# A fused decoder layer: an opening ordered engine by engine, the output bias added by VectorE, and products nobody reads in three recurring waits of TensorE

## The reference

```python
x = x + attn(layernorm(x))                       # one head, width 128, softmax over 256 keys
x = x + xattn(layernorm(x), ctx)                 # 16 heads of 64, 1601 keys; out @ Wo + bo
x = x + ffn_block(layernorm(x))                  # a router takes 31 of 256 rows of each batch
```

```python
q = (x @ Wq).reshape(B, Nq, 16, 64)              # k, v likewise from the context
sim = einsum('bhid,bhjd->bhij', q, k) * SCALE
attn = softmax(sim)
return einsum('bhij,bhjd->bhid', attn, v).reshape(B, Nq, 1024) @ Wo + bo
```

## Time and profile before

| | |
|---|---|
| median of 3 executions | 2245.14 us (2243.27 to 2247.11) |
| the profiled execution: its own time | 2249.61 us |
| its span, first to last instruction | 2248.4 us |
| mean granted TensorE clock | 0.989 |
| busy: PE / ACT / POOL / DVE | 2154.0 / 1831.9 / 1926.4 / 1781.7 us |
| the first score product starts at | 41.00 us |

### The profile page before, as it was taken

The page is one execution under the profiler, slowest core; times in us unless marked ns, Lnnn a source line. Parts: engine busy times, 40 slices in busy tenths (PEclk is TensorE's granted clock), DMA queues, the critical chain, the costliest instruction groups (busy, mean ns, idle before and its releaser), DMA issues.

```text
span 2248.4 us, 58064 instructions
## 1 busy us (share of the span) xinstructions
PE 2154.0 (96%) x22151; PEld 1574.0 (70%) x22151; DVE 1781.7 (79%) x3728; ACT 1831.9 (81%) x3125; POOL 1926.4 (86%) x1112
## 2 busy tenths in 40 slices
PE   7899999999999999999999999999999999999998
PEld 4677777777777767777777777767777777676665
DVE  6777888787887888878787788877868788886755
ACT  5888888888888888888788887888878888888862
POOL 2799999999998989898898898888978898898982
PEclk9999999999999999999999999999989999999999
DMA  3110000000000000000000000000000000000000
GB/s 69 37 43 13 2 9 5 2 13 2 13 2 4 11 2 13 2 13 2 11 13 2 13 2 2 13 2 13 2 11 12 2 13 2 2 1 2 2 8 13
DMA packets 17221, 22.15 MB, mean 10 GB/s; under 512 B 5601, under 2 KB 14834, under 8 KB 16946
## 3 DMA queue, kind: packets, MB, share of 16 engines
q1 hardware_dynamic: 15842, 18.24, 3.0%
q10 hardware_dynamic: 1104, 0.20, 0.1%
HBM read 16.20 MB, written 2.10 MB: 8 GB/s over the span
## 4 chain that ended last, share of the span: by engine, by line
PE 68%; DVE 12%; ACT 10%; issue 8%; POOL 3%; DVEq 0%; ACTq 0%; POOLq 0%
PE PS L541 12%; PE PS L579 12%; PE PS L542 11%; PE PS L558 10%; PE PS L560 9%; PE PS L605 4%; DVE EH L1042 4%; ACT PF L860 3%; DVE over L1065 3%; POOL EL L1512 2%; ACT EH L867 2%; ACT over L882 2%; PE PS L589 2%; PE PS L615 2%; DVE junk L1308 1%
## 5 line engine op out<-in xcount | busy, mean ns | idle before, releaser
L1512 POOL TENSOR_TENSOR EL<-PF,EH 124x1024 f16<-124x1024 f32 x828 | 1760.8, 2149 | 229.1 <-DVE EH L1042 111.2
L860 ACT ACTIVATE PF<-PS 124x512 f32<-124x512 f32 x1664 | 973.9, 603 | 251.5 <-PE PS L542 240.4
L558 PE MATMUL PS<-Ch,EH 123*128 123x97 f16 (+1 forms) x6656 | 769.8, 208 | 22.0 <-POOL EL L1512 11.2
L560 PE MATMUL PS<-Cl,EL 123*128 123x97 f16 (+1 forms) x6656 | 766.5, 208 | 0.0
L1042 DVE TENSOR_SCALAR_CACHE_REDUCE EH<-PF 124x1024 f16<-124x1024 f32 x621 | 745.1, 1209 | 9.2 <-ACT PF L860 9.0
L558 PEld LDWEIGHTS PS<-Ch,EH 123*128 123x128 f16 (+1 forms) x6656 | 611.4, 98 | 186.7 <-issue 61.1
L560 PEld LDWEIGHTS PS<-Cl,EL 123*128 123x128 f16 (+1 forms) x6656 | 600.8, 98 | 171.6 <-issue 4.6
L1065 DVE CUSTOM_DVE_ANT_1 over<-over,PS 128x806 f32<-128x806 f32 x512 | 506.0, 988 | 200.0 <-ACT over L882 110.8
L541 PE MATMUL PS<-AH,ChT 97*124 97x512 f16 x1664 | 649.6, 390 | 9.9 <-ACT PF L860 5.8
L542 PE MATMUL PS<-AL,ClT 96*124 96x512 f16 x1664 | 637.1, 383 | 0.0
L882 ACT ACTIVATE over<-PS 128x806 f32<-128x806 f32 x512 | 434.4, 848 | 36.1 <-PE PS L579 15.5
(11 more groups left out here) (234 smaller groups left out, 1816.2 us busy)
## 6 DMA issues: line engine op xcount, KB each, us to landing
Cf<-in_ctx SPq DMA_DIRECT2D x16, 546.0 KB
X<-in_x SPq DMA_DIRECT2D x16, 128.0 KB, 2.5
out_x<-X SPq DMA_DIRECT2D x16, 128.0 KB, 1.7
msk<-in_attention_mask SPq DMA_DIRECT2D x4, 256.0 KB, 4.3
AH<-mh SPq DMA_DIRECT2D x63, 2.0 KB
Cf<-in_ctx SPq DMA_DIRECT2D x16, 53.6 KB
xWqT<-in_xWqT SPq DMA_DIRECT2D x2, 256.0 KB, 7.5
xWo<-in_xWo SPq DMA_DIRECT2D x2, 256.0 KB, 4.2
```

Source lines behind the costliest of these rows:

```text
L558: pe.matmul(PS[:, 6, u0:u0 + DC + 1], EH[0:kr, r, qs], Ch[j][0:kr, t, :], start=(t == 0 and q == 0), stop=False, skip_group_check=True)
L560: m = pe.matmul(PS[:, 6, u0:u0 + DC + 1], EL[0:kr, r, qs], Cl[j][0:kr, t, :], start=False, stop=(t == KT - 1), skip_group_check=True)
L860: act.activation(PF[:, n % PRING, :], PS[0:KP, 4 + n % 2, :], ACT.Exp).then_inc(sg("ex"), 1)
L1512: pool.tensor_tensor(EL[:, r - 1:r + 1, :], PF[:, f - 1:f + 1, :], EH[:, r - 1:r + 1, :], ALU.subtract).then_inc(sg("lo_pool"), 1)
```

## The change

It has four parts. The opening has an order for each engine instead of one for all, the four `gm` groups that make `M` go into it out of the first four places of the stream (their banks change with that), two small loads are issued ahead of two large ones, and POOL's fill of two rows waits for the angle steps of DVE. The bias `xbo` is loaded to all 128 partitions and added to `X` by DVE in a step of its own (`bias`), once for each batch, after the second norm has read `X`; line 603 and its row of ones go. In the stream, PE issues 7, 11 and 3 products of the identity ahead of `("base", 4 * gq + 6, 7)`, `("c_thid", gq)` and `("c_scat", gq, 0)`, for the three groups beside the stream: 21 for a group, 63 in all. They go to the bank that the next scores use and wait for the same exponential. And the products nobody reads in the opening are given out anew, with nine of them between the products of the first folds.

```diff
     if b == 0:
-        todo += [(k, ("gm", q, part)) for k, (q, part) in enumerate(((0, 2), (0, 3), (1, 2), (1, 3)))]
...
+        todo += [(q[6] + 2, ("bias", n))]
...
+def opening(engine):
+    stats, norm, turn, qk, val, sc, probs, att, stats1, norm1, x2 = self_attention(0)
+    high, low = context_of(0)[:2], context_of(0)[2:]
+    turns = transposes_of(0)
+    folds = [maximum(0, ht) for ht in range(4)]
+    moved = [("gm", q, part) for q, part in ((0, 2), (0, 3), (1, 2), (1, 3))]
+    if engine == "pe":
+        out = [turn, qk, ("wvo",), sc, ("sigma", 0), ("gm", 0, 0), ("gm", 0, 1), val, probs, ("gtop", 0), att]
+        out += turns[:2] + [("gm", 1, 0), ("gm", 1, 1), ("load_ctx", 1), x2, ("q", 0, 0)] + folds[0] + folds[1] + [("gtop", 1)]
+        out += folds[2] + folds[3] + turns[2:3] + moved[:1]
+        return out + [("placemax", 0, 0, 2)] + moved[1:2] + turns[3:] + moved[2:3] + [("q", 0, 1)] + moved[3:]
+    if engine == "act":
+        out = [turn, ("trig",), qk, sc, probs] + high + [("gsplit", 0)] + turns[:2] + [x2, ("q", 0, 0)]
+        out += [f[0] for f in folds] + [("gsplit", 1)] + turns[2:3]
+        return out + [("placemax", 0, 0, 2)] + turns[3:] + [("q", 0, 1)]
+    if engine == "dve":
+        out = [stats, norm, ("trig",), qk, ("ctx_max", 0), ("wvo",), sc, ("sigma", 0), ("gmax", 0), ("ctx_scale", 0), val]
+        out += [("gtop", 0), att, stats1, ("gsplit", 0), norm1, ("keys", 0), x2] + low + [("q", 0, 0)]
+        out += folds[0] + [("gmax", 1)] + folds[1] + [("gtop", 1)] + folds[2] + folds[3]
+        return out + [("gsplit", 1)] + moved[:3] + [("q", 0, 1)] + moved[3:] + [("bias", 0)]
+    return [stats, ("consts",), ("more_consts",), stats1]
...
-        xbo = sb("xbo", [1, P])
-        ones = sb("ones", [1, P])
+        xbo = sb("xbo", [P, P])
...
-        GM_BANKS = ((2, 3, 6, 6), (4, 5, 6, 6))
+        GM_BANKS = ((2, 3, 6, 0), (4, 5, 2, 6))
...
+        STREAM_BUSY = {}
+        for gq in range(NG - 1):
+            STREAM_BUSY |= {("base", 4 * gq + 6, 7): 7, ("c_thid", gq): 11, ("c_scat", gq, 0): 3}
...
+            def keep_busy_until_scores(n, *step):
+                w.wait_ge(sg("ex"), n - 1)
+                for _ in range(STREAM_BUSY[step]):
+                    pe.matmul(PS[:, 4 + n % 2, :], identb[:, :], wide, start=True, stop=True)
...
+                scored += k == "st"
+                if (k, *s.a) in STREAM_BUSY:
+                    keep_busy_until_scores(scored, k, *s.a)
...
+                    if i == 5:
+                        w.wait_ge(sg("m_done"), 3 if k == "diff" else 2)
...
-                        if qd == 0:
-                            w.wait_ge(sg("in_xbo"), 16)
-                            pe.matmul(PS[:, kb, t * D:(t + 1) * D], ones[0:1, :], xbo[0:1, :], start=True, stop=False)
                         for c in range(QC):
                             m = pe.matmul(PS[:, kb, t * D:(t + 1) * D], UT[:, t, c, :], M[:, qd * QC + c, :],
-                                          start=(c == 0 and qd > 0), stop=(c == QC - 1))
+                                          start=(c == 0), stop=(c == QC - 1))
...
+                elif k == "bias":
+                    b, = s.a
+                    w.wait_ge(sg("xn2"), i)
+                    w.wait_ge(sg("in_xbo"), 16)
+                    dve.tensor_tensor(X[:, T * b:T * b + T, :], X[:, T * b:T * b + T, :],
+                                      xbo[:, :].rearrange("p (o d) -> p o d", o=1).to_broadcast([P, T, D]),
+                                      ALU.add).then_inc(sg("bo_added"), 1)
...
                     const_ready()
+                    w.wait_ge(sg("trig_in"), 1)
                     for j in range(2):
                         const(pool.memset(ChT[j][DC:DC + 1, :, :], SHIFT_ROW))
```

More of the change, by code:

```diff
@@ L169, in plan @@
         split = AV_LAG + 17 * (b == 0)
-        todo += [(split + 0, ("ctx_hi", n, 0)), (split - 1, ("ctx_hi", n, 1))]
+        todo += [(split, ("ctx_hi", n, 0)), (split - 1, ("ctx_hi", n, 1))]
         todo += [(split + 4, ("ctx_lo", n, 0)), (split + 8, ("ctx_lo", n, 1))]
@@ L184, in put @@
         stream.append((n + shift.get(kind, 0), len(stream), (kind, *a)))
-    first = self_attention(0)
-    turns = transposes_of(0)
-    out += [first[0], ("consts",), *first[1:3], ("trig",), first[3], ("wvo",), ("ctx_max", 0), first[5], first[4]]
-    out += [("gm", 0, 0), ("gm", 0, 1), ("gmax", 0), ("sigma", 0), ("gtop", 0)]
-    split = context_of(0)
-    out += [first[6], ("more_consts",), ("ctx_scale", 0), first[7], first[8]] + split[:2]
-    out += [("gsplit", 0), split[2]] + turns[:2] + [("gm", 1, 0), ("gm", 1, 1)]
-    out += [first[9], split[3], ("load_ctx", 1), first[10], ("keys", 0), ("gmax", 1), ("q", 0, 0)]
-    out += maximum(0, 0)[:2] + [("gtop", 1)] + maximum(0, 0)[2:] + maximum(0, 1) + maximum(0, 2) + maximum(0, 3) + turns[2:3]
-    out += [("placemax", 0, 0, 2)] + turns[3:] + [("gsplit", 1), ("q", 0, 1)]
+    out += opening(engine)
     groups, todo = beside_plan(), []
@@ L422, in build @@
                     for of in (((2 * m, 0),), ((2 * m, P), (2 * m + 1, -64)), ((2 * m + 1, 64),))]
-        CONST_IDENT, CONST_TURNS, CONST_ALL = 5, 13, 29
+        CONST_IDENT, CONST_TURNS, CONST_ALL = 5, 12, 28
         HALVES = (slice(0, 7), slice(7, KT))
-        BUSY = {("sa_t", 0): 8, ("sa_qk", 0): 1, ("sa_turn", 0): 3, ("sa_o", 0): 2,
-                ("ctx_t", 0, 0, 0, 7): 2, ("sa_f", 0): 4, ("q", 0, 0): 4, ("diff", 0, 0): 3,
-                ("placemax", 0, 0, 2): 5,
+        BUSY = {("sa_t", 0): 9, ("sa_qk", 0): 2, ("sa_o", 0): 1, ("sa_f", 0): 4, ("q", 0, 0): 4, ("diff", 0, 0): 3,
+                ("diff", 0, 1): 2, ("base", 0, 1): 2, ("base", 0, 2): 2, ("base", 0, 3): 3,
                 ("turn_u", B - 1, QD - 1, 0): 4, ("proj", B - 1, QD - 1): 1, ("sel_row", B - 1): 17,
@@ L433, in build @@
                 ("c_scat", NG - 1, 0): 2}
-        BUSY_LATER = (("sa_f", 0), ("q", 0, 0), ("diff", 0, 0), ("placemax", 0, 0, 2))
+        STREAM_BUSY = {}
+        for gq in range(NG - 1):
+            STREAM_BUSY |= {("base", 4 * gq + 6, 7): 7, ("c_thid", gq): 11, ("c_scat", gq, 0): 3}
+        BUSY_LATER = (("sa_f", 0), ("q", 0, 0), *((k, 0, ht) for k in ("diff", "base") for ht in range(4)))
         order = whole_order("pe")
@@ L520, in keep_busy @@
                     pe.matmul(PS[:, bank, :], identb[:, :], wide, start=True, stop=True)
+            def keep_busy_until_scores(n, *step):
+                w.wait_ge(sg("ex"), n - 1)
+                for _ in range(STREAM_BUSY[step]):
+                    pe.matmul(PS[:, 4 + n % 2, :], identb[:, :], wide, start=True, stop=True)
+            scored = 0
             for s in order:
@@ L714, in tensor_program @@
                             w.wait_ge(*last_of_head(6))
+                        elif (q, part) == (0, 3):
+                            w.wait_ge(sg("fold"), 4)
+                        elif (q, part) == (1, 2):
+                            w.wait_ge(sg("relu"), 4)
                         else:
-                            w.wait_ge(sg("m_done"), 2 * q + part - 2)
+                            w.wait_ge(sg("m_done"), 1)
                         for c in range(QC):
@@ L1104, in vector_program @@
                     w.wait_ge(sg("pj_mm"), i)
+                    w.wait_ge(sg("bo_added"), b + 1)
                     w.wait_ge(sg("pj_x"), i - 1)
@@ L1467, in pool_program @@
                 if k == "consts":
-                    const(pool.memset(ones[:, :], 1.0), pool.memset(lower[:, :, :, :], 1.0), pool.memset(headmask[:, :], 1.0),
+                    const(pool.memset(lower[:, :, :, :], 1.0), pool.memset(headmask[:, :], 1.0),
                           pool.memset(blockmask[:, :], 1.0))
@@ L1562, in sync_program @@
             load_x(0)
+            for j, n in enumerate(("b_q", "b_k")):
+                sp.dma_start(cols[:, j:j + 1], a[n].rearrange("(p o) -> p o", o=1)).then_inc(sg("in_wqk"), 16)
             for n, t in (("w_qT", wqT), ("w_kT", wkT)):
                 sp.dma_start(t[:, :], a[n]).then_inc(sg("in_wqk"), 16)
-            for j, n in enumerate(("b_q", "b_k")):
-                sp.dma_start(cols[:, j:j + 1], a[n].rearrange("(p o) -> p o", o=1)).then_inc(sg("in_wqk"), 16)
             load_context(0)
@@ L1572, in sync_program @@
                                  a[n].rearrange("(j p) n -> p j n", p=P)[:, halves[q], :]).then_inc(sg(f"in_xg{q}"), 16)
-            sp.dma_start(xbo[:, :], a["xbo"].rearrange("(o n) -> o n", o=1)).then_inc(sg("in_xbo"), 16)
+            sp.dma_start(xbo[:, :], row("xbo")).then_inc(sg("in_xbo"), 16)
             load_x(1)
```

## The result

The changed kernel takes **2213.52 us** (median of 4 runs, 2211.51 to 2214.06) and the kernel before 2244.20 us in the same rounds (median of 4, 2240.58 to 2247.11). The ratio is 0.9862, with a 95% interval of 0.9845 to 0.9880, so the change makes the kernel 1.4% faster, some 31 us. The profiled execution after took 2211.51 us, with a span of 2210.3 us. The forecast was 2210 us with a range of 2200 to 2223.

What follows compares the result with a forecast made beforehand. PE was taken to bound the kernel (busy 2154.0 of 2248.4 us). From the profiled 2249.6 us, -17.3 + 0.5 - 14 - 6.5 gave 2212.3, lowered to 2210 us for excess low clock; range 2200 to 2223, 8 times in 10.

Steps and rivals of the forecast that it cites:

- The bound and the bias products: PE bounds; first projections without line 603's products each save 1.15 us on PE, -17.3 us in all (-18.4 to about -5).
- The added step on DVE: Bias addition on DVE ahead of the fold: nothing on PE expected, +0.5 us put in, bounds 0 and 8.
- the bound from below: Least length of one bias addition on DVE: 0.42 us, from an addition of the same shape with one operand in PSUM.
- The slower rival: Each of 15 adds blocks behind a POOL low half, 2.6 us on PE's path: 39 us, 2251 us; chance 0.03.
- The products nobody reads: 63 extra PE products in three waits per group keep the clock up: -14 us, between 0 and -18.
- the clock's term: The -14 us for low clock avoided in the stream: 13.5 us at the first five places, 0.5 us at the sixth.
- The last place: Sixth low-clock stretch, at 2177 us: 10.3 us would cost 4.5 us, counted 0.5 us as POOL sets the pace there.
- the clock falls anyway: What is left of each wait, with narrow `c_scat` products behind it, lowers the clock: 10 us lost, 2220 us; chance 0.20.
- the signs of being wrong: Clock still falling behind `c_scat`, low-half waits growing behind projections, or batches' stretches shortening by less than 1.15 us.
- The opening: First score product at about 37.3 instead of 41.00, 3.7 us, plus 3.6 us among scores; -6.5 us taken, bounds -2 and -9.
- the four groups: The `M` groups no longer stand between the first scores, where each takes 0.9 us: 3.6 us more.
- The sum: 2249.6 - 17.3 + 0.5 - 14 - 6.5 = 2212.3 us; half of the profiled run's 4.5 us excess off gives 2210 us.

Runs made afterwards that it cites:

- the second addition: Changed kernel with another addition of the same shape behind each bias addition, into a buffer nobody reads: 2233.48 us, ratio 0.9947.

## Why the prediction was right, and which terms were not

**The bound and the bias products**: right. The first projection takes 1.45 us, a batch without low clock is 1.15 to 1.20 us shorter, and PE's waits for POOL's low halves came to 12.3 us in all after 11.2 before: 17.3 us, as summed; by medians 17.6 and 19.1 us.

**The added step on DVE**: no cost on PE, and 0.5 us was in the sum for it. The mechanism was as reckoned, the wait for the end of a low half of POOL, but the fold is 1.2 us late and not 1.7: 12 of the 16 additions take 1.27 us, as the low half is nearer to its end when they begin; one takes 1.55 us and the last 0.47, and the two first, with POOL idle, take 0.41 us, the bound from below. That a batch gained the whole 1.15 us is what shows the addition to be free. I judged `base` to be 0.6 us later than a fold that is 1.7 us late. With a fold 1.2 us late, 1.1 us would be left, and the second addition measured 1.3 us at that product: the cover was sized rightly. The rule of the Trainium skill that I cited, SBUF — State Buffer (which ops grab the shared pair), agrees: 1.27 us beside POOL and 0.41 without it, and one column beside POOL still 0.86 in the mean. The slower rival had the right mechanism, blocked additions. Its turning point of 2.5 us a batch was not reached, but twice the work on DVE at this place loses 1.65 us a batch and takes 20 of the 31 us away.

**The products nobody reads**: the mechanism was right, the size was not. The step that failed is "The first five places have 6.7 + 3 x 3.4 + 13.7 = 30.6 us of it and cost 13.5 us". Between the two profiled executions it is right (13.0 us); as a forecast of medians it is not. Runs of before range from 2239 to 2255 us, the three other profiles without the products have 17 to 24 us of low clock in the stream, where this one had 41, partly in other places, and the medians give 4.4 us for the products, 9.0 us in the variant without the addition. The profiled execution of before was 4.5 us above its median; I wrote that this would be low clock in excess "which is counted already" and took off half. It should have come off the clock's term: what one execution lost by the clock is a draw, not a rate. The price of 0.44 us for each us of low clock roughly stood up: at the third scattering 3.9 us came back for 10.2 us, 0.38 each, and the slowest and the fastest run of before are 16.4 us apart for 45 us, 0.37 each. At 0.38 the 15 us that the products take away make 5.7 us.

**The last place** was priced at 0.5 us because "PE's wait is longer than three products". That was right, and it even got worse: 3.35 us are left after three products, where before waited 1.91 us without any. Two rows of the timeline of before:

```profile
2173.36 2.27 DVE L1422 TENSOR_SCALAR XA<-XA,XS 128x128 f32<-128x128 f32 x1
...
2175.68 0.71 PE L834 MATMUL PS<-XA,KX 32*128 32x128 f32 x4 [1.91 <-DVE XA L1422]
```

After the change DVE's step there, `XA<-XA,XS`, started at 2133.82, in the middle of five low halves of POOL, and took 4.37 us. Two rows of the changed kernel:

```profile
2133.82 4.37 DVE L1459 TENSOR_SCALAR XA<-XA,XS 128x128 f32<-128x128 f32 x1
...
2127.62 10.47 POOL L1550 TENSOR_TENSOR EL<-PF,EH 124x1024 f16<-124x1024 f32 x5
```

It ends at 2138.19, with the last of the five (2127.62 + 10.47 = 2138.09). This is the 1.9 us given back. The products are not its cause: the step takes 4.35 to 4.38 us in eleven of the twelve further profiles (2.28 us in the other), also with the opening alone and with the addition alone. The rival "the clock falls anyway" came true at this one place and nowhere else in the stream, and with it one of the signs of being wrong that I had named, low clock behind `c_scat`.

**The opening** was under-sized: 8.9 us between the profiles and 9.2 to 10.7 us by medians, for -6.5. The step that failed is "I get the fourth fold at about 32.8 instead of 35.5": it ended at 31.7, and the turned maxima stood at 32.09 instead of my 33.5; the three groups behind them took the 3.7 us that I had (3.8), so the first score product is 1.5 us ahead of my 37.3. The first nine tiles gave 3.8 us, near the 3.6 priced for the four groups, of which I had withheld some. But I gave no price to the clock in the opening, and two windows of the kernel before show it low there:

```profile
24.00:40.00 16.00, 11.37 (x53) 4.82 (x50) 8.27 (x22) 7.13 (x11) 0.00 (x0) 0.79 0.13 39
40.00:80.00 40.00, 36.32 (x285) 25.38 (x286) 31.99 (x69) 29.70 (x53) 22.59 (x13) 0.96 0.04 12
```

That is 10 us at the lower level (6.8 us from 30.8 and 3.4 us from 41.0 on), and the changed kernel's profile has none there. At 0.44 us each this is an estimated 4.5 us of the 8.9 us, 1.5 of them in the first tiles, so the agreement with the 3.6 us is in part luck; no run separates clock from order here. Against it, in five of eleven profiles the clock falls between 12.5 and 14.5 us, and in four of these it costs 2 to 2.5 us of the gain, which the profile of before doesn't show and I did not foresee.

**The sum**: 2212.3 us on the basis of the profiled execution, and the profiled one after took 2211.5. Opening (2.4 more) and the clock with what it gave back (11.1 instead of 14) came out even there, which is luck. The median came out 3.5 us above the forecast. For medians the clock's term was 9.6 us too large (4.4 instead of 14, or 5.0 by the variant with 9.0); the opening and the bias with its addition gave 2.7 and 2.3 us more than their terms, and the base, 2249.6 us less half of 4.5, stood 3.1 us above the median of before. These offset one another, so that the forecast came this near is luck too; that each part gains, and why, is not.

**Left open**: why the same wait lowers the clock in one group or execution and not in another; whether what is left between the products' worth of 4.4 and 9.0 us is a true interaction with the addition; how the gain is shared among the three places, which was not tried; how much of the opening's gain is clock.

## What to carry to other kernels

What the clock cost in one profiled execution is a draw: look at the range of the runs and of their mean clocks, and book only what returns in all of them. Products nobody reads were worth having where they filled the wait to its end, cost their full length beyond it, and did nothing for the clock in most executions where 1.4 us of the wait were left; so count the wait at each place by itself. Without the products the last group's wait ahead of the scattering was 4.0 us in three of four profiles, and the others' 0.86 us. Moving work from the engine that bounds to one with slack is safe only as long as the slack *at that place* lasts: one addition per batch was free here, two took two thirds of the whole gain.

## What the runs showed of the hardware

- An addition on DVE with both inputs in SBUF takes 0.41 us with POOL idle and 1.27 or 2.35 us beside POOL's low halves, and one of a single column 0.86 us in the mean (0.15 at the least): its length is set by where it falls in POOL's list, for it ends with or 0.3 us behind a low half.
- A DVE operation of 128x128 that starts in the middle of POOL's back-to-back low halves took 4.37 us, the length of two of them, and ended with the last of the five. For the addition I had taken one low half waited for, 2.2 us, as the most.
- A wait of 1.04 us for `pmax`, as 13 batches of the kernel with two additions have it, lowered the clock in no batch of its profile; its mean clock is 0.997. The wait of 0.86 us ahead of the narrow scattering products did so in both of the first two groups of before, and in neither of them in the kernel without the 63 products. So the length of a wait alone does not tell whether the clock falls; what else does is not shown.
- Over eleven executions of one kernel, before, the mean clock went from 0.984 to 0.994 and the time from 2255.4 to 2238.9 us, about 0.37 us for each us at the lower level.
